# DLRM tower on one core: fifteen tables picked by matmul in place of fourteen, and eight buffers for gathered rows

## The chip, the cores and the metric

One core of one Trainium2 chip. The metric is the device time of one execution in microseconds (us), lower is better. A profiled execution gives a span, from its first to its last recorded instruction, and its own time.

## The reference

For each of 512 samples, 32 rows of 128 numbers are looked up in 32 tables by `ids`. All pairs of these rows are multiplied (a 32 x 32 matrix of dots for a sample, of which the upper triangle is used), 16 context numbers are added, and three layers follow.

```python
e = jnp.stack([tbl_0[ids[:, 0]], ..., tbl_31[ids[:, 31]]], axis=1)   # 512 x 32 x 128
dot = jnp.einsum('bnd,bmd->bnm', e, e)
z = dot[:, iu, ju]                                   # iu, ju = triu_indices(32, k=1)
h = jnp.concatenate([z, dense_ctx], axis=1)          # 512 x 512
h = jnp.maximum(h @ W_top1 + b_top1, 0.0)            # 512 x 512
h = jnp.maximum(h @ W_top2 + b_top2, 0.0)            # 512 x 256
y = h @ W_top3
```

Eleven tables have 1000 rows, twelve have 1250, eight 12500 and one 125000. Everything is float32.

## The kernel before

The embeddings end in `emb`, with the 128 dimensions on the partitions, by one of two ways.

**Picks.** The 14 smallest tables (`PICK`) are read whole, as 8 chunks of 128 rows each (11 tables) or 10 chunks (3 tables), 118 chunks in all. For each chunk there is a mask `onehot`, 128 rows x 512 samples, that is one where a sample's id is that row. TensorE multiplies the chunk by its mask and adds the chunks of a table up in a bank of `two_ps` (L479, L481). A table is split in two parts, `high` and `low`, each multiplied by itself: ScalarE copies `high` (L353), VectorE subtracts `low` = table - high (L275, "the subtraction"). Most masks are made by VectorE (L290, three or four chunks to an instruction), some by ScalarE in two steps, `away` (L373) and `onehot` (L383); the table `BY_ACT` says how many of each table. `onehot` holds 16 chunks, so a mask waits until TensorE has counted up `picked_done` for the chunk that held its place. `pick_out` on ScalarE copies two tables at a time out of `two_ps` when the second is complete. Three tables are held, and SyncE loads the next one (`home<-picked`) when the one three before has been subtracted.

**Gathers.** The other 18 features (`GF`) come as single rows. GpSimd issues an indirect DMA for each tile of 128 rows (L266, 72 of them). The samples are in 4 blocks of 128; a block has 5 banks of tiles, the first of `MORE` = 2 tiles and four of 4 tiles, 20 banks in all (`NB`). TensorE turns a bank by transposes, `turn(k)` (L495), into `turn_ps`, and ScalarE copies it to `emb` (`emb_out(k)`, L353), which counts up `emb_ready`. The tile `rows` holds `ROWS_HELD` = 4 banks: before the gathers of bank k GpSimd waits until `turned` has reached k - 3. In TensorE's order, after the picks of table t comes `turn(t - 1)`, up to bank 12, and behind it bank 13.

**Dots.** For each pair of samples one matmul of 64 columns (L519; the profile has two records for each) gives their 32 x 32 dots. There are 8 groups of 64 samples (64 records each), two to a block, going to `free_ps` and `two_ps` in turn. `dots_out` copies them to `home`, ScalarE the first half of a group and VectorE the second (L179). SyncE stores a block's dots to HBM (`dots_store`, L183) and loads them back as `pairs` (L189), 128 features and context on the partitions.

**Layers.** `layer1(r)` (L528) wants the pairs of block r, and four blocks are put through layer 1, then layers 2 and 3 in three parts. Between them stand the last banks' turns and the dots of groups 6 and 7.

All engines' lists are written by hand, in the order in which the code below stands; they meet by semaphores only.

Of the kernel before, what the change touches and what calls it, by code (L numbers as in the profile page):

```python
# [7 lines left out]
        1250, 12500, 1250, 1250, 1250, 12500, 12500, 1000, 1000, 1000, 1250, 1250, 1000, 1000,  # L8
        1000, 1250, 1250, 1250]

PICK = 14
PICKED = sorted(range(F), key=lambda f: (ROWS[f], f))[:PICK]
GATHERED = [f for f in range(F) if f not in PICKED]
SLOTS = GATHERED + PICKED
# [2 lines left out]
KRMAX = max(KR)  # L17
CHUNK0 = [sum(KR[:t]) for t in range(PICK + 1)]
STEPS = sorted(set(KR))
# [1 line left out]
PIECE = 2  # L21
PIECES0 = KR[0] // PIECE

BY_ACT = [0, 2, 2, 2, 1, 2, 2, 2, 2, 1, 2, 2, 2, 3]

TWOS = -(-PICK // 2)
ACT0 = [sum(BY_ACT[:t]) for t in range(PICK + 1)]

# [8 lines left out]
NB = BLOCKS * BANKS  # L37
TILES = [TB if k % BANKS else MORE for k in range(NB)]
TILE0 = [sum(TILES[:k]) for k in range(NB + 1)]

TURNED = PICK - 1
TABLES_HELD, IDS_HELD, HOT, AWAY, ROWS_HELD = 3, 4, 16, 6, 4

BATCH = 4

# [11 lines left out]
def build(nc, row_ids, pick_ids, tables, picked, context, w1, w2, small, y):  # L57
# [4 lines left out]
    with ctx:  # L62
# [6 lines left out]
        def sem(name):  # L69
            return ctx.enter_context(nc.semaphore(name))  # L70
# [53 lines left out]
        row_ids_in = sem("row_ids_in")  # L124
        pick_ids_in = [sem(f"pick_ids_in{t}") for t in range(PICK)]
        piece_in = [sem(f"piece_in{j}") for j in range(PIECES0)]
# [17 lines left out]
        turned = sem("turned")  # L144
# [31 lines left out]
        def copy_dots(copy, grp, j):  # L176

            at = GRP // 4 * (grp % 2) + GRP // 8 * j
            return copy(dot_sb[:, grp // 2 % 2, :, at:at + GRP // 8],  # L179
                        dot_ps[grp % 2][j][:, :].rearrange("p (g c) -> p c g", c=2 * F))  # L180
# [71 lines left out]
        @block.gpsimd  # L252
        def _(pool):
            for i, k in enumerate(STEPS):
                pool.iota(own_row_i[:, i, 0:k], [[1, k]], base=0, channel_multiplier=k).then_inc(own_rows_made, 1)
            pool.memset(ident[:, :], 0.0).then_inc(ident_ready, 1)
            pool.wait_ge(ident_ready, 1)
            pool.affine_select(out=ident[:, :], in_=ident[:, :], compare_op=ALU.not_equal, fill=1.0,
                               base=0, pattern=[[-1, P]], channel_multiplier=1).then_inc(ident_ready, 1)
            pool.wait_ge(row_no_ready, 1)  # L260
            for k in range(NB):
                if k >= ROWS_HELD:
                    pool.wait_ge(turned, k - ROWS_HELD + 1)
                for i in range(TILES[k]):
                    c = TILE0[k] + i
                    pool.indirect_dma_start(  # L266
                        rows[:, k % ROWS_HELD, i, :], None, tables,
                        bass.IndirectOffsetOnAxis(ap=row_no[:, c:c + 1], axis=0)
                    ).then_inc(rows_in[k % ROWS_HELD], 16)

        @block.vector
        def _(dve):
# [5 lines left out]
            def make_onehots(t, k0, k1):  # L278

                i, k = STEPS.index(KR[t]), k0  # L280
                while k < k1:
                    c = CHUNK0[t] + k
                    n = min(BATCH, k1 - k, HOT - c % HOT)
                    if k1 - k == BATCH + 2:
                        n = min(n, 3)
                    if c + n > HOT:
                        dve.wait_ge(picked_done, c + n - HOT)
                    ids = pick_id[:, t % IDS_HELD, :].unsqueeze(1).broadcast_to([P, n, B])
                    own = own_ps[:, i, k:k + n].unsqueeze(2).broadcast_to([P, n, B])
                    dve.tensor_tensor(onehot[:, c % HOT:c % HOT + n, :], ids, own, ALU.is_equal).then_inc(onehot_dve, n)  # L290
                    k += n
# [19 lines left out]
            for j in range(PIECES0):  # L311
                make_onehots(0, PIECE * j, min(PIECE * (j + 1), KR[0] - BY_ACT[0]))
                dve.wait_ge(high_ready, j + 1)
                split_low(0, PIECE * D * j, PIECE * D * (j + 1))
            for t in range(1, PICK):
# [4 lines left out]
                dve.wait_ge(pick_ids_in[t], 16)  # L320
                make_onehots(t, 0, KR[t] - BY_ACT[t])

# [28 lines left out]
        def _(act):  # L351
# [13 lines left out]
            def make_away(t):  # L365

                i, first = STEPS.index(KR[t]), KR[t] - BY_ACT[t]
                act.wait_ge(pick_ids_in[t], 16)
# [23 lines left out]
            def emb_out(k):  # L392
                act.wait_ge(turned, k + 1)
                r, u = divmod(k, BANKS)
                if u == 0:
                    out = emb[:, BLK * r:BLK * (r + 1), 4 * TB:GF]
                    in_ = turn_ps[k % 2][:, 0:MORE * P].rearrange("p (f b) -> p b f", f=MORE)
                else:
                    b0 = BLK * r + SUB * (u - 1)
                    out = emb[:, b0:b0 + SUB, 0:4 * TB].rearrange("p b (i f) -> p i b f", i=TB)  # L400
                    in_ = turn_ps[k % 2][:, :].rearrange("p (i b f) -> p i b f", i=TB, f=4)
                copy(out, in_).then_inc(emb_ready, 1)

            def dots_out(grp):
                act.wait_ge(dots, 2 * grp + 1)
                if grp >= 4:
                    act.wait_ge(dots_stored[grp // 2 - 2], 64)
                copy_dots(copy, grp, 0).then_inc(dots_act, 1)
# [18 lines left out]
                    make_away(t + 3)  # L427
                    split_high(t + 3)
            emb_out(TURNED)
            dots_out(0)  # L430
            dots_out(1)
            emb_out(TURNED + 1)
            for grp in range(2, 6):
                dots_out(grp)
            for k in range(TURNED + 2, NB - 1):
                emb_out(k)
# [26 lines left out]
        def _(pe):  # L463
            def pick(t):
# [4 lines left out]
                at, out = t % TABLES_HELD, two_ps[t // 2 % 2][:, t % 2, :]  # L469
                own = KR[t] - BY_ACT[t]  # L470
                for k in range(KR[t]):
# [12 lines left out]
            def turn(k):  # L484
                pe.wait_ge(rows_in[k % ROWS_HELD], 16 * sum(TILES[k % ROWS_HELD:k + 1:ROWS_HELD]))
                if k >= 2:
                    pe.wait_ge(emb_ready, k - 1)
                if k == NB - 1:
                    pe.wait_ge(emb_ready, k)
                for i in range(TILES[k]):  # L490
                    bank, at = k % 2, i
                    if k == NB - 1:

                        bank, at = (k + i // 2) % 2, i % 2
                    last = pe.transpose(turn_ps[bank][:, at * P:(at + 1) * P], rows[:, k % ROWS_HELD, i, :], ident[:, :])  # L495
                last.then_inc(turned, 1)
# [25 lines left out]
            def dot_group(grp):  # L522
                dot(grp, 0)
                dot(grp, 1)
# [24 lines left out]
            for t in range(PICK):  # L549
                pick(t)  # L550
                if t:
                    turn(t - 1)
            turn(TURNED)
            pe.wait_ge(pick_emb_ready, TWOS)
            dot_group(0)
            dot_group(1)
            turn(TURNED + 1)
            for grp in range(2, 6):
                dot_group(grp)
            turn(NB - 5)  # L560
            turn(NB - 4)
            pe.wait_ge(weights_in, 64)
            layer1(0)
# [99 lines left out]
```

## Time and profile before

| | |
|---|---|
| Median of 3 runs | 150.77 us (150.52 to 151.89) |
| Profiled execution's own time | 150.31 us |
| Its span | 148.5 us |
| TensorE busy, matmuls (PE) | 119.0 us, 1008 instructions |
| TensorE busy, weight loads (PEld) | 96.8 us |
| VectorE (DVE) busy | 81.2 us |
| ScalarE (ACT) busy | 68.6 us |
| GpSimd (POOL) busy | 76.0 us |
| Mean granted TensorE clock | 0.94 |

Busy times of engines overlap. Matmuls are pipelined and their ends are modelled, so the sum of their durations is more than the time in which they run. "Record" below is one matmul instruction in the trace.

### The profile page before, as it was taken

To read this page: it belongs to the slowest core of one execution; us is meant where nothing else is said; L and a number is where in the kernel's file an instruction comes from. 1 tells how busy PE (TensorE), PEld (TensorE's weight loads), DVE (VectorE), ACT (ScalarE), POOL (GpSimd) and SP (SyncE) were. 2 spreads that over 40 slices of the span, in tenths; PEclk is the share of its full clock that TensorE was granted. 3 is DMA by queue.
4 is the path that set the end of the run, shared out by engine and by line. 5 is a ranking of instruction groups with operands and counts; after the bars stand their busy time and mean duration, and the time that the engine had idled before them with its cause. 6 is when DMAs were issued, how large, how long until landed. Compare 5 with 4: busy or idle time off the path is not lost.

```text
span 148.5 us, 2544 instructions
## 1 busy us (share of the span) xinstructions
PE 119.0 (80%) x1008; PEld 96.8 (65%) x1008; DVE 81.2 (55%) x80; ACT 68.6 (46%) x109; POOL 76.0 (51%) x80
## 2 busy tenths in 40 slices
PE   0195998789999989769599764487499989799993
PEld 0174776476777776545488564276499979699971
DVE  1599997899999999676993000020113041313300
ACT  3359806989998974069961051012024040300032
POOL 3777885747788777848777567506301700000000
PEclk9999999999999999999779969559869999999999
DMA  2797776557647868882212112205425733042000
GB/s 64 187 338 240 283 214 194 124 160 216 206 121 176 272 226 246 233 288 53 53 35 53 53 33 57 53 2 126 114 63 130 188 99 73 4 141 71 4 0 1
DMA packets 10990, 19.29 MB, mean 130 GB/s; under 512 B 2385, under 2 KB 7377, under 8 KB 10978
## 3 DMA queue, kind: packets, MB, share of 16 engines
q1 hardware_dynamic: 8290, 14.01, 32.0%
q0 software_dynamic: 2304, 4.72, 11.6%
q10 hardware_dynamic: 384, 0.39, 0.8%
q8 instruction: 8, 0.13, 0.4%
q14 instruction: 4, 0.03, 0.1%
HBM read 17.02 MB, written 2.13 MB: 129 GB/s over the span
## 4 chain that ended last, share of the span: by engine, by line
PE 65%; issue 14%; DVE 12%; another core or an unknown queue 4%; ACT 2%; DMA 1%; DVEq 0%
PE two_ps L479 16%; PE two_ps L481 13%; DVE onehot L290 9%; PE two_ps L519 8%; PE two_ps L528 8%; PE free_ps L519 7%; PE turn_ps L495 5%; PE free_ps L539 3%; DVE low L275 3%; PE two_ps L539 2%; ACT emb L353 2%; PE two_ps L544 1%; DMA id_sb<-row_ids 1%; PE turn_ps L528 1%
## 5 line engine op out<-in xcount | busy, mean ns | idle before, releaser
L266 POOL DMA_INDIRECT rows<-tables,row_no x72 | 75.1, 1044 | 42.3 <-issue 19.5
L479 PE MATMUL two_ps<-onehot,high 128*128 128x512 f32 x118 | 50.7, 430 | 15.5 <-DVE low L275 6.9
L290 DVE TENSOR_TENSOR onehot<-pick_id,free_ps 128x1536 fp32r<-128x1536 int16 (+2 forms) x30 | 53.1, 1800 | 4.2 <-DMA pick_id<-pick_ids 2.1
L481 PE MATMUL two_ps<-onehot,low 128*128 128x512 f32 x118 | 48.4, 410 | 0.0
L479 PEld LDWEIGHTS two_ps<-onehot,high 128*128 128x128 f32 x118 | 23.5, 199 | 27.0 <-issue 21.1
L481 PEld LDWEIGHTS two_ps<-onehot,low 128*128 128x128 f32 x118 | 23.5, 199 | 4.4
L275 DVE TENSOR_TENSOR low<-home,high 128x1024 fp32r<-128x1024 f32 (+2 forms) x17 | 18.3, 1076 | 3.0 <-ACT high L353 1.6
L519 PE MATMUL two_ps<-emb 128*64 128x64 f32 x240 | 12.8, 263 | 7.8 <-issue 6.8
L353 ACT ACTIVATE high<-home 128x1024 fp32r<-128x1024 f32 (+2 forms) x17 | 15.8, 941 | 4.9 <-DMA home<-picked 4.2
L373 ACT ACTIVATE away<-pick_id,less_row 128x512 f16<-128x512 int16 x25 | 16.7, 715 | 1.4 <-DMA pick_id<-pick_ids 1.4
L179 DVE COPY home<-free_ps 128x512 f32<-128x512 f32 x4 | 2.8, 692 | 26.4 <-remote 24.1
L519 PEld LDWEIGHTS two_ps<-emb 128*64 128x64 f32 x240 | 11.1, 173 | 9.1 <-issue 8.0
L353 ACT ACTIVATE emb<-two_ps 128x1024 f32<-128x1024 f32 x7 | 7.8, 1110 | 18.2 <-remote 12.9
L353 ACT ACTIVATE emb<-turn_ps 128x512 f32<-128x512 f32 (+1 forms) x20 | 10.6, 542 | 11.6 <-PE turn_ps L495 10.9
L519 PE MATMUL free_ps<-emb 128*64 128x64 f32 x272 | 12.1, 249 | 3.6 <-ACT emb L353 2.4
L383 ACT ACTIVATE onehot<-away 128x512 fp32r<-128x512 f16 x25 | 14.3, 622 | 0.0
L519 PEld LDWEIGHTS free_ps<-emb 128*64 128x64 f32 x272 | 11.0, 162 | 4.8 <-ACT emb L353 2.9
L528 PE MATMUL two_ps<-pairs,w_sb 128*128 128x128 f32 x104 | 12.5, 277 | 0.0
L294 DVE TENSOR_SCALAR h<-two_ps,small_sb 128x128 f32<-128x128 f32 x15 | 4.3, 344 | 14.4 <-PE two_ps L528 7.8
L528 PEld LDWEIGHTS two_ps<-pairs,w_sb 128*128 128x128 f32 x104 | 11.9, 192 | 0.1
L495 PE MATMUL turn_ps<-ident,rows 128*128 128x128 f32 x72 | 10.9, 276 | 0.0
L353 ACT ACTIVATE home<-two_ps 128x512 f32<-128x512 f32 x4 | 2.4, 597 | 18.1 <-PE two_ps L519 18.1
(32 smaller groups left out, 46.4 us busy)
## 6 DMA issues: line engine op xcount, KB each, us to landing
home<-picked SPq DMA_DIRECT2D x10, 512.0 KB
home<-picked SPq DMA_DIRECT2D x3, 640.0 KB
pick_id<-pick_ids SPq DMA_DIRECT2D x14, 128.0 KB
dot_out<-home SPq DMA_DIRECT2D x14, 128.0 KB, 2.5
w_sb<-w SPq DMA_DIRECT2D x3, 512.0 KB
rows<-tables,row_no POOLq DMA_INDIRECT x72
pairs<-dot_out SPq DMA_DIRECT2D x14, 64.0 KB, 2.0
home<-picked SPq DMA_DIRECT2D x4, 128.0 KB, 3.9
```

Source lines behind the costliest of these rows:

```text
L266: pool.indirect_dma_start(rows[:, k % ROWS_HELD, i, :], None, tables, bass.IndirectOffsetOnAxis(ap=row_no[:, c:c + 1], axis=0)).then_inc(r ...
L275: dve.tensor_tensor(low[:, at, a:b], table[:, at, a:b], high[:, at, a:b], ALU.subtract).then_inc(low_ready, 1)
L290: dve.tensor_tensor(onehot[:, c % HOT:c % HOT + n, :], ids, own, ALU.is_equal).then_inc(onehot_dve, n)
L353: return act.activation(out, in_, ACT.Copy)
L373: act.activation(away[:, m % AWAY, :], pick_id[:, t % IDS_HELD, :], ACT.Abs, bias=less_row[:, i, k:k + 1]).then_inc(away_ready, 1)
L383: act.activation(onehot[:, c % HOT, :], away[:, m % AWAY, :], ACT.Relu, bias=1.0, scale=-1.0).then_inc(onehot_act, 1)
L479: pe.matmul(out, high[:, at, D * k:D * (k + 1)], onehot[:, c % HOT, :], start=(k == 0), stop=False)
L481: pe.matmul(out, low[:, at, D * k:D * (k + 1)], onehot[:, c % HOT, :], start=False, stop=(k == KR[t] - 1)).then_inc(picked_done, 1)
L495: last = pe.transpose(turn_ps[bank][:, at * P:(at + 1) * P], rows[:, k % ROWS_HELD, i, :], ident[:, :])
L519: last = pe.matmul(out, e, e, start=True, stop=True, tile_position=(0, 64 * h))
L528: last = pe.matmul(h1_ps[r][n], w1_sb[:, c, n * P:(n + 1) * P], pairs[:, r:r + 1, :, c, :], start=(c == 0), stop=(c == PC - 1))
L539: return pe.matmul(h2_ps[part][n], w2_sb[:, c, n * P:(n + 1) * P], h1[:, c, samples(part)], start=(c == 0), stop=(c == N1 - 1))
```

## The change

- The 15 smallest tables are picked: a fourth one of 10 chunks joins, 128 chunks in all. 17 features are gathered, so the first bank of each block has one tile, and there are 68 gathers. `BY_ACT` gets an entry; table 12 gives one more mask to ScalarE, table 13 one fewer. `TWOS` becomes 8, and with it the banks in `two_ps` that dots and layers use swap places.
- `rows` holds 8 banks. GpSimd's gate is four banks behind up to bank 15 (the same as before); banks 16 to 19 wait only until 12 banks are turned.
- Bank 14 is turned behind the picks of the last table with bank 13 ahead of it, and bank 15 follows; then the dots of groups 0 to 5 stand in a row, where before bank 14's turn stood between groups 1 and 2, and bank 15's behind group 5.

```diff
--- before.py
+++ after.py
@@ -8,7 +8,7 @@
         1250, 12500, 1250, 1250, 1250, 12500, 12500, 1000, 1000, 1000, 1250, 1250, 1000, 1000,
         1000, 1250, 1250, 1250]
 
-PICK = 14
+PICK = 15
 PICKED = sorted(range(F), key=lambda f: (ROWS[f], f))[:PICK]
 GATHERED = [f for f in range(F) if f not in PICKED]
 SLOTS = GATHERED + PICKED
@@ -21,7 +21,7 @@
 PIECE = 2
 PIECES0 = KR[0] // PIECE
 
-BY_ACT = [0, 2, 2, 2, 1, 2, 2, 2, 2, 1, 2, 2, 2, 3]
+BY_ACT = [0, 2, 2, 2, 1, 2, 2, 2, 2, 1, 2, 2, 3, 2, 3]
 
 TWOS = -(-PICK // 2)
 ACT0 = [sum(BY_ACT[:t]) for t in range(PICK + 1)]
@@ -39,7 +39,9 @@
 TILE0 = [sum(TILES[:k]) for k in range(NB + 1)]
 
 TURNED = PICK - 1
-TABLES_HELD, IDS_HELD, HOT, AWAY, ROWS_HELD = 3, 4, 16, 6, 4
+TABLES_HELD, IDS_HELD, HOT, AWAY, ROWS_HELD = 3, 4, 16, 6, 8
+
+AHEAD = 4
 
 BATCH = 4
 
@@ -259,8 +261,8 @@
                                base=0, pattern=[[-1, P]], channel_multiplier=1).then_inc(ident_ready, 1)
             pool.wait_ge(row_no_ready, 1)
             for k in range(NB):
-                if k >= ROWS_HELD:
-                    pool.wait_ge(turned, k - ROWS_HELD + 1)
+                if k >= AHEAD:
+                    pool.wait_ge(turned, min(k - AHEAD + 1, max(PICK - 3, k - ROWS_HELD + 1)))
                 for i in range(TILES[k]):
                     c = TILE0[k] + i
                     pool.indirect_dma_start(
@@ -427,10 +429,8 @@
                     make_away(t + 3)
                     split_high(t + 3)
             emb_out(TURNED)
-            dots_out(0)
-            dots_out(1)
             emb_out(TURNED + 1)
-            for grp in range(2, 6):
+            for grp in range(6):
                 dots_out(grp)
             for k in range(TURNED + 2, NB - 1):
                 emb_out(k)
@@ -551,13 +551,10 @@
                 if t:
                     turn(t - 1)
             turn(TURNED)
+            turn(TURNED + 1)
             pe.wait_ge(pick_emb_ready, TWOS)
-            dot_group(0)
-            dot_group(1)
-            turn(TURNED + 1)
-            for grp in range(2, 6):
+            for grp in range(6):
                 dot_group(grp)
-            turn(NB - 5)
             turn(NB - 4)
             pe.wait_ge(weights_in, 64)
             layer1(0)
```

TensorE, behind the last chunk of the last table's picks, before (numbers behind names are buffers; of each turn and each half group of dots the first row stands, not the x3 or x15 that repeat it):

```order
L495 MATMUL turn_ps0<-ident,rows 128x128 [waits emb_ready,rows_in0]
L495 MATMUL turn_ps1<-ident,rows 128x128 [waits emb_ready,rows_in1]
L519 MATMUL free_ps0<-emb 64x64 [waits emb_ready,pick_emb_ready]
L519 MATMUL free_ps1<-emb 64x64 [waits emb_ready]
L519 MATMUL two_ps1<-emb 64x64 [waits emb_ready]
L495 MATMUL turn_ps0<-ident,rows 128x128 [waits emb_ready,rows_in2]
L519 MATMUL free_ps0<-emb 64x64 [waits dots_act,emb_ready]
```

and after:

```order
L495 MATMUL turn_ps1<-ident,rows 128x128 [waits emb_ready,rows_in5]
L495 MATMUL turn_ps0<-ident,rows 128x128 [waits emb_ready,rows_in6]
L495 MATMUL turn_ps1<-ident,rows 128x128 [waits emb_ready,rows_in7]
L519 MATMUL free_ps0<-emb 64x64 [waits emb_ready,pick_emb_ready]
L519 MATMUL free_ps1<-emb 64x64 [waits emb_ready]
L519 MATMUL two_ps0<-emb 64x64 [waits emb_ready]
L519 MATMUL free_ps0<-emb 64x64 [waits dots_act,emb_ready]
```

Three turns (banks 13, 14 and 15) now stand ahead of the first dot where there were two (12 and 13), and none between groups 1 and 2.

VectorE, the last picks, before:

```order
L290 TENSOR_TENSOR onehot<-pick_id,free_ps 128x2048 [waits picked_done]
L275 TENSOR_TENSOR low<-home,high 128x1280 [waits picked_done,high_ready]
L290 TENSOR_TENSOR onehot<-pick_id,free_ps 128x2048 [waits picked_done,pick_ids_in13]
L290 TENSOR_TENSOR onehot<-pick_id,free_ps 128x1536 [waits picked_done]
L179 COPY home<-free_ps 128x64x8 [waits dots]
```

and after:

```order
L277 TENSOR_TENSOR low<-home,high 128x1280 [waits picked_done,high_ready]
L292 TENSOR_TENSOR onehot<-pick_id,free_ps 128x2048 [waits picked_done,pick_ids_in14]
L292 TENSOR_TENSOR onehot<-pick_id,free_ps 128x1536 [waits picked_done]
L181 COPY home<-free_ps 128x64x8 [waits dots]
L181 COPY home<-two_ps 128x64x8 [waits dots]
```

A subtraction and two mask instructions (seven chunks) are added ahead of the first copy of dots.

## Rows read from the trace of the kernel before

**Rows 1.** the page's part 4, the chain by engine.

```profile
PE 65%; issue 14%; DVE 12%; another core or an unknown queue 4%; ACT 2%; DMA 1%; DVEq 0%
```

**Rows 2.** VectorE's timeline: start us, duration us, engine, line, out<-in, [idle before <-releaser].

```profile
61.44 2.29 DVE L290 TENSOR_TENSOR onehot<-pick_id,free_ps 128x2048 fp32r<-128x2048 int16 x1 [1.13 <-PE two_ps L481]
64.30 2.29 DVE L290 TENSOR_TENSOR onehot<-pick_id,free_ps 128x2048 fp32r<-128x2048 int16 x1 [0.57 <-remote]
68.23 1.49 DVE L275 TENSOR_TENSOR low<-home,high 128x1280 fp32r<-128x1280 f32 x1 [1.65 <-ACT high L353]
...
74.04 1.48 DVE L275 TENSOR_TENSOR low<-home,high 128x1280 fp32r<-128x1280 f32 x1
75.44 3.94 DVE L290 TENSOR_TENSOR onehot<-pick_id,free_ps 128x2048 fp32r<-128x2048 int16 x2
97.28 0.69 DVE L179 COPY home<-free_ps 128x512 f32<-128x512 f32 x1 [17.90 <-remote]
```

**Rows 3.** ScalarE's timeline, the same columns.

```profile
64.23 1.14 ACT L353 ACTIVATE emb<-two_ps 128x1024 f32<-128x1024 f32 x1 [6.79 <-remote]
...
78.93 0.60 ACT L353 ACTIVATE emb<-turn_ps 128x512 f32<-128x512 f32 x1 [2.36 <-PE turn_ps L495]
85.62 1.02 ACT L353 ACTIVATE emb<-two_ps 128x1024 f32<-128x1024 f32 x1 [6.10 <-remote]
...
120.20 1.09 ACT L353 ACTIVATE emb<-turn_ps 128x512 f32<-128x512 f32 x2 [5.04 <-PE turn_ps L495]
```

**Rows 4.** TensorE's timeline, around the picks.

```profile
56.66 0.60 PE L495 MATMUL turn_ps<-ident,rows 128*128 128x128 f32 x4
...
83.06 0.39 PE L481 MATMUL two_ps<-onehot,low 128*128 128x512 f32 x1
```

**Rows 5.** windows: stretch, us, then busy us of each engine, granted clock, DMA share, GB/s.

```profile
72.00:76.00 4.00, 3.93 (x11) 3.09 (x12) 4.00 (x3) 4.00 (x8) 3.30 (x3) 0.59 0.19 49
```

**Rows 6.** the chain that ended last, in order of time: start us, us, what.

```profile
86.70 3.54 PE free_ps L519 x63
90.35 1.06 issue
...
97.17 2.63 PE two_ps L519 x44
...
102.51 0.37 issue
...
106.52 3.12 PE two_ps L519 x57
...
113.72 0.81 PE turn_ps L495 x6
...
120.85 1.15 PE free_ps L519 x32
```

**Rows 7.** GpSimd's timeline.

```profile
65.19 0.94 POOL L266 DMA_INDIRECT rows<-tables,row_no  x1 [1.55 <-remote]
...
68.93 1.61 POOL L266 DMA_INDIRECT rows<-tables,row_no  x1 [0.30 <-issue]
...
85.92 0.94 POOL L266 DMA_INDIRECT rows<-tables,row_no  x1 [2.08 <-PE turn_ps L495]
...
94.66 0.94 POOL L266 DMA_INDIRECT rows<-tables,row_no  x1 [0.31 <-issue]
100.79 0.95 POOL L266 DMA_INDIRECT rows<-tables,row_no  x1 [5.19 <-PE turn_ps L495]
...
104.54 0.95 POOL L266 DMA_INDIRECT rows<-tables,row_no  x1 [0.30 <-issue]
...
118.11 0.94 POOL L266 DMA_INDIRECT rows<-tables,row_no  x1 [0.30 <-issue]
```

**Rows 8.** SyncE's queue, its timeline.

```profile
60.00 0.43 SPq L236 DMA_DIRECT2D w_sb<-w  x1
...
114.59 1.74 SPq L189 DMA_DIRECT2D pairs<-dot_out  x4
```

## Prediction, made before the changed kernel was run

> **What bounds the kernel now.** I read the chain of work that ended last by engine first, then the timelines of VectorE, ScalarE, TensorE and GpSimd from 56 to 122 us. The chain is 65% TensorE, but 14% is "issue", time in which an engine waited for nothing that the profile shows, and 4% an unknown releaser [rows 1]. So TensorE's list of work is the path, with holes in it, and the question is what makes the holes. There are three stages.
>
> Up to 83.45 us the picks run at VectorE's pace. A ten-chunk table costs it one subtraction of 1.48 us and seven or eight masks: table 13 runs from 74.04 to 75.44 + 3.94 = 79.38, which is 5.34 us for the subtraction and seven masks [rows 2]. Before that VectorE idled for 1.13, 0.57 and 1.65 us [rows 2]; the last is a wait for ScalarE, which had sat 6.79 us in front of its copy out of `two_ps` [rows 3]. That copy waits only for TensorE's count of table 9, and TensorE had done table 9 before the turn at 56.66 us [rows 4]. The count got out 7 us late.
>
> From 83.45 to 113.72 us stand the dots of three blocks, 384 records. The first 63 take 3.54 us. Then come holes of 1.06 us and the like with at most 5 records between two, until 97.17: 18 records in 6.8 us. A second set begins at 102.51 and ends at 106.52; after it 57 and twice 64 records run without a hole to 113.72, 0.039 us each [rows 6]. GpSimd's rows stand beside this: its gathers run from 85.92 to 95.60 and from 100.79 to 105.49 [rows 7]. The holes end 1.57 and 1.03 us after the last gather of each run. Between 97.17 and 102.51, mostly without gathers, there is no hole. Counts are late in the same places: VectorE's first copy of dots waited 17.90 us and began at 97.28 [rows 2], though the first 63 records were executed by 90.24. I read this as one effect: while gathers follow each other without a pause, what TensorE reports can get out slowly, and after some 64 dense records TensorE itself stands. The cause I can't see; that the two go together I can.
>
> From 113.72 us on comes a tail of 34.8 us, dense on TensorE but for one place: ScalarE's copy of bank 17 began at 120.20 after 5.04 us of waiting [rows 3], and half of the dots of group 6 had to stand behind it until 120.85 [rows 6]. Gathers ran until 119.05 there [rows 7].
>
> **The change, part by part.**
> *One more table.* VectorE gets +5.34 us (the same subtraction and seven masks; tables 12 and 13 swap one mask). Against it: TensorE now ends 4.1 us after VectorE's last mask, since after an idle start it ran partly at the lower clock of 1.2 GHz (granted clock 0.59 between 72 and 76 us, [rows 5]). At 2.4 GHz a chunk takes 0.46 us, its two matmuls of 0.23 (the last of the picks, at 83.06, is released into the turn at 83.29, [rows 4]), and six chunks follow the last mask, 2.8 us, so 1.3 comes back. The idle 3.35 us before table 12 may shrink by nothing or by nearly all of it: with banks 0, 5 and 10 one tile shorter, GpSimd reaches its pauses 1.25 to 4 us earlier, and late counts come out with a pause. Bounds for the end of the picks are thus +0.7 and +4.0; I take +2.5, the end nearer to the pile-up seen, so 86.0.
>
> *Handing over.* Ahead of the first dot TensorE now needs ScalarE's pick copy of one table, its copy of bank 13 and a one-tile turn: about 0.6 (a bank's copy, [rows 3]) + 0.6 + 0.3, against 1.02 for the pair of tables now. With the 2 us by which the count is late (83.45 to 85.62, [rows 3]) I put 3.5 where it was 3.25. The dots start at 89.5, where it was 86.70.
>
> *The gathers.* Each costs 0.94 us and 0.30 before the next, 1.25. Of the 80.6 us between the first, at 3.28, and 83.84 (2.08 before 85.92, [rows 7]), 3.8 are three pauses like the one before 65.19, 70.0 are 56 gathers, and the other 6.8 come from gathers that overlap a subtraction and take 1.6 us or more, as at 68.93. For 68: 3.3 + 85.0 + 6.8 + 0.7 for the new subtraction is 95.8 without a pause. The gates for banks 4, 6 and 12 are the old ones and cost 1.3 us each when they bite; bank 15 needs turn 11. With one to three pauses the gathers end between 97.1 and 99.7; with a late gate at bank 15, later still. I take 99.0. Behind that gate nothing pauses them: banks 16 to 19 have buffers of their own.
>
> A rule on the new subtraction: the gather at 68.93, which meets the subtraction of 68.23 to 69.72, takes 0.67 us more than the others [rows 2, 7]. The Trainium skill ("SBUF — State Buffer", Who interferes with whom) says that a VectorE instruction with two inputs in SBUF and a GpSimd one that reads SBUF shut each other out wholly. By it the price could be up to the whole 1.48 us, and the gathers' end 99.8. The trace, where most of that subtraction is waited out, agrees.
>
> *The dots.* From 89.5 the first 64 records need 3.6 us, to 93.1. Then the slow flow until 99.0 + 1.3 = 100.3: 7.2 us at 18 per 6.8 us, 19 records. Of the other 301 the first 44 go at 0.060 us as they do after the first set of holes (2.63 us for 44, [rows 6]) and 257 at 0.039, together 12.7. The dots end at 113.0, against 113.72 now, with turn 14 among them: **-0.7**. The start hardly matters here. A microsecond later costs 2.6 records, 0.1 us, as long as the dots start before 96. It is the gathers' end plus 14.0 us that sets it.
>
> *The turn before layer 1.* Six transposes in 0.81 us (bank 15's pair and bank 16, [rows 6]) become four: **-0.25**.
>
> *The tail.* No gather runs beside it any more. Bank 17's copy can follow its turn, over at 118.5, at once, as bank 11's did at 78.93 [rows 3, 4]; the second half of the dots of group 6 can begin at 119.6 in place of 120.85: **-1.25**. The rest is TensorE's own work and stays, if the pairs arrive: the load for the second block is issued from 114.59 [rows 8], 7.4 us ahead of its use at 122.0, and shifts with the dots.
>
> Buffers for eight banks cost no time. The new table's 640 KB and mask ids ride on SyncE's queue ahead of the weights, whose last load is issued at 60.00 [rows 8] and is used after 113: 50 us of cover.
>
> **Sum:** -0.7 - 0.25 - 1.25 = -2.2; the pause at bank 6 may fall away with the shorter bank 5, for which I take 0.3 more: -2.5. The span goes from 148.5 to 146.0, the profiled execution's own time from 150.31 to 147.8, and the median, now 0.46 above that, to **148.3 us**.
>
> **The rivals.**
> *Late counts throttle the picks (slower).* Between 63.6 and 83.8 us TensorE idled for some 4 us and ran slowly for 3, so little piled up. The changed kernel has four ten-chunk tables there and no pause. In the slow flow a chunk is reported every 0.7 us (VectorE's releases at 61.44 and 64.30 stand four chunks apart, [rows 2]) where it is executed in 0.46. If that holds, VectorE stalls for free masks, turn 11 comes late, and bank 15's gate opens at 82 where 77 is due. Then 17 gathers of 1.27 end at 103.6 and the dots at 117.6: +3.9 - 1.5, so 153.2 us. It decides from a gate later than 79.6; there the loss has eaten the tail's gain. For it: the 7 us of delay at 57 to 64. Against it: from 65.19 to 79 us gathers ran without a pause and bank 11's copy was still prompt [rows 3].
>
> *The holes belong to the dots, not to the gathers.* Dense, 384 records take 64 x 0.056 + 320 x 0.039 = 16.1 us; the 27.0 us of now hold 0.7 of a turn and 10.2 of loss. If that comes whatever GpSimd does, the dots end at 89.5 + 26.3 = 115.8, the tail's late copy stays, and with -0.25 this is 152.6 us, or 150.8 with the picks at their lower bound. Against it: 185 records without a hole once the gathers were over. The Trainium skill, in the section named above, says that PE never waits on anyone at these ports. By that rule the gathers would have no hold on TensorE; the trace's two sets of holes stand against it.
>
> *No holes at all.* Both sets began 4.4 and 1.7 us after GpSimd had started again behind a wait. If the restart is the trigger, gathers that run on don't hurt. The dots then take 16.1 us from 89.5, to 105.6: -8.1 - 1.5, so 141.2 us. For it: 32 to 53 us, where gathers ran on beside dense picks. Against it: nothing shows that dots go as picks do.
>
> **How the numbers follow.** A measurement of this kernel tells about 1%, 1.5 us, from no change. The forecast has a chance of 0.50 and a range of its own of 146.4 to 150.3 (the gathers' end at 97.1 to 101); 0.38 of it lies under 149.3. Late counts in the picks get 0.20, holes that belong to the dots 0.13, of which nearly half is within 1%, and no holes 0.17, nearly all of it faster. That makes 0.55 faster, 0.20 within 1%, 0.25 slower. The range reaches into the outer cases on both sides: 143.0 to 153.0.
>
> **What the profile of the changed kernel would show.** If I am right: the picks end near 86, the gathers near 99 without a pause from about 77, holes between the dots until a microsecond after the last gather and none after, the dots over at 113, the copy of bank 17 prompt. I am wrong if holes go on after the gathers or are missing beside them, if bank 15's gate opens after 80, or if the pairs of a block arrive later than TensorE asks for them.

## The result, and the profile after

The changed kernel took 155.0 us in the median of 4 runs (154.38 to 156.27), the kernel before 151.33 us beside it: a ratio of 1.0255, 95% interval 1.0162 to 1.0347. It is slower: the whole interval lies above 1, though it reaches below 1.02. Ratios, here and below, compare only runs in the faster of two states that executions of one kernel show, so they can differ a little from the quotient of the medians. The profiled execution took 154.84 us, with a span of 153.0.

From the page of the changed kernel, the granted clock in 40 slices and the chain by engine (the counterparts of [rows 1, 5]):

```profile
PEclk9998699999999999999999965555699999999999
...
PE 48%; DVE 20%; another core or an unknown queue 13%; issue 8%; DMA 4%; ACT 3%; SPq 2%; DVEq 0%
```

The chain has lost TensorE (65% to 48%) and gained an unknown releaser (4% to 13%, 20 us). The clock is at its lower level of 1.2 GHz (0.5) from some 92 to 107 us: TensorE was busy for 1.1 us of the 19 from 85.75 to 104.8.

VectorE's timeline (counterpart of [rows 2]):

```profile
75.39 1.48 DVE L277 TENSOR_TENSOR low<-home,high 128x1280 fp32r<-128x1280 f32 x1
76.79 3.94 DVE L292 TENSOR_TENSOR onehot<-pick_id,free_ps 128x2048 fp32r<-128x2048 int16 x2
108.91 0.69 DVE L181 COPY home<-free_ps 128x512 f32<-128x512 f32 x1 [28.18 <-PE free_ps L519]
```

The masks end at 76.79 + 3.94 = 80.73, 4.0 us sooner than the 79.38 + 5.34 = 84.72 that the added work alone would give: the 3.35 us of idle time that VectorE had before table 12 are gone. Then it stands for 28.18 us until the first dots.

ScalarE's (counterpart of [rows 3]):

```profile
78.07 0.60 ACT L355 ACTIVATE emb<-turn_ps 128x512 f32<-128x512 f32 x1 [3.40 <-remote]
...
88.15 1.02 ACT L355 ACTIVATE emb<-two_ps 128x1024 f32<-128x1024 f32 x1 [6.70 <-remote]
93.09 0.60 ACT L355 ACTIVATE emb<-turn_ps 128x512 f32<-128x512 f32 x1 [3.91 <-remote]
103.21 1.02 ACT L355 ACTIVATE emb<-two_ps 128x512 f32<-128x512 f32 x1 [9.53 <-remote]
104.04 1.64 ACT L355 ACTIVATE emb<-turn_ps 128x512 f32<-128x512 f32 x3
...
124.14 1.08 ACT L355 ACTIVATE emb<-turn_ps 128x512 f32<-128x512 f32 x2 [4.23 <-PE turn_ps L495]
```

These are the rows to look at. 78.07 is the copy of bank 11, 88.15 that of tables 12 and 13, 93.09 that of bank 12, 103.21 that of the last table, 104.04 those of banks 13 to 15, 124.14 those of banks 17 and 18. TensorE's own rows (counterparts of [rows 4, 6]):

```profile
83.64 0.39 PE L481 MATMUL two_ps<-onehot,low 128*128 128x512 f32 x1
...
93.83 1.08 PE L495 MATMUL turn_ps<-ident,rows 128*128 128x128 f32 x4 [8.10 <-issue]
104.81 0.45 PE L495 MATMUL turn_ps<-ident,rows 128*128 128x128 f32 x1 [9.89 <-ACT emb L355]
105.18 3.68 PE L519 MATMUL free_ps<-emb 128*64 128x64 f32 x64
108.65 2.58 PE L519 MATMUL two_ps<-emb 128*64 128x64 f32 x64
111.06 2.03 PE L519 MATMUL free_ps<-emb 128*64 128x64 f32 x64
...
118.62 0.66 PE L495 MATMUL turn_ps<-ident,rows 128*128 128x128 f32 x4
119.86 3.81 PE L528 MATMUL two_ps<-pairs,w_sb 128*128 128x128 f32 x32 [0.58 <-DMA pairs<-dot_out]
...
124.47 2.08 PE L519 MATMUL free_ps<-emb 128*64 128x64 f32 x64
```

The last chunk was executed at 83.64 to 84.03; its count reached ScalarE at 103.2, **19 us later**. Table 13 was done at 78.4, and was seen at 88.1, 9.7 us late; bank 12, turned at 79.0, was seen at 93.1, 14 us late. It began earlier: bank 11 was turned from 72.78 to 73.38, and ScalarE saw that at 78.07, 4.7 us late. TensorE has next to nothing to do meanwhile: bank 14's turn at 93.83 waits for the copy at 93.09, and bank 15's at 104.81 for bank 13's copy, the first of those at 104.04, which stands behind the one of 103.21 in ScalarE's list. GpSimd's timeline (counterpart of [rows 7]):

```profile
54.92 1.18 POOL L268 DMA_INDIRECT rows<-tables,row_no  x1 [1.32 <-remote]
...
78.30 0.94 POOL L268 DMA_INDIRECT rows<-tables,row_no  x1 [0.61 <-remote]
...
98.28 0.94 POOL L268 DMA_INDIRECT rows<-tables,row_no  x1 [0.30 <-issue]
```

From 54.92 on the gathers follow each other 0.30 us apart. The one exception is bank 15's gate: it waits for bank 11's late count too, and opened at 78.30 after 0.61 us. The last gather ended at 99.22, and the last count came out 4 us after that. The dots then ran without one hole, from 105.18 to 118.62. The four parts of the span, before and after:

| us | before | after |
|---|---|---|
| until the end of the picks | 83.45 | 84.03 |
| from there to the first dot | 3.25 | 21.15 |
| dots of three blocks | 27.02 | 13.44 |
| the rest | 34.78 | 34.38 |
| span | 148.5 | 153.0 |

### The profile page after: what moved, and what is told of

Same layout as the page of the kernel before. It is cut to its first block, busy times and chain, and to the rows that moved or that the text cites. A ratio compares the mean times of both kernels' runs of the same rounds, so it can differ in the third digit from the quotient of the medians.

```text
span 153.0 us, 2595 instructions
## 1 busy us (share of the span) xinstructions
PE 117.5 (77%) x1024; PEld 96.8 (63%) x1024; DVE 86.3 (56%) x83; ACT 76.4 (50%) x117; POOL 73.1 (48%) x76
## 4 chain that ended last, share of the span: by engine, by line
PE 48%; DVE 20%; another core or an unknown queue 13%; issue 8%; DMA 4%; ACT 3%; SPq 2%; DVEq 0%
DVE onehot L292 15%; PE two_ps L479 12%; PE two_ps L481 11%; PE two_ps L528 8%; DVE low L277 5%; PE free_ps L519 4%; PE free_ps L539 3%; PE two_ps L519 3%; PE turn_ps L495 2%; ACT emb L355 2%; PE two_ps L539 2%; DMA dot_out<-home 1%; DMA pairs<-dot_out 1%; PE two_ps L544 1%
## 5 line engine op out<-in xcount | busy, mean ns | idle before, releaser
L268 POOL DMA_INDIRECT rows<-tables,row_no x68 | 72.2, 1062 | 25.4 <-issue 18.9
L479 PE MATMUL two_ps<-onehot,high 128*128 128x512 f32 x128 | 54.4, 425 | 12.3 <-DVE low L277 6.1
L292 DVE TENSOR_TENSOR onehot<-pick_id,free_ps 128x1536 fp32r<-128x1536 int16 (+2 forms) x32 | 56.9, 1812 | 1.6 <-DMA pick_id<-pick_ids 1.3
L481 PE MATMUL two_ps<-onehot,low 128*128 128x512 f32 x128 | 52.1, 407 | 0.0
L481 PEld LDWEIGHTS two_ps<-onehot,low 128*128 128x128 f32 x128 | 25.5, 199 | 4.9
L495 PEld LDWEIGHTS turn_ps<-ident,rows 128*128 128x128 f32 x68 | 8.6, 145 | 21.4 <-issue 19.9
L355 ACT ACTIVATE emb<-two_ps 128x1024 f32<-128x1024 f32 (+1 forms) x8 | 11.4, 1425 | 19.1 <-remote 16.2
L355 ACT ACTIVATE emb<-turn_ps 128x512 f32<-128x512 f32 (+2 forms) x20 | 10.8, 553 | 16.9 <-remote 11.6
L385 ACT ACTIVATE onehot<-away 128x512 fp32r<-128x512 f16 x28 | 16.1, 623 | 1.0 <-PE two_ps L481 1.0
L519 PE MATMUL two_ps<-emb 128*64 128x64 f32 x240 | 8.5, 231 | 1.0 <-ACT emb L355 1.0
L519 PEld LDWEIGHTS two_ps<-emb 128*64 128x64 f32 x240 | 8.0, 147 | 1.3 <-ACT emb L355 1.1
```

The lines of the kernel that those rows point to most:

```text
L268: pool.indirect_dma_start(rows[:, k % ROWS_HELD, i, :], None, tables, bass.IndirectOffsetOnAxis(ap=row_no[:, c:c + 1], axis=0)).then_inc(r ...
L355: return act.activation(out, in_, ACT.Copy)
L385: act.activation(onehot[:, c % HOT, :], away[:, m % AWAY, :], ACT.Relu, bias=1.0, scale=-1.0).then_inc(onehot_act, 1)
L479: pe.matmul(out, high[:, at, D * k:D * (k + 1)], onehot[:, c % HOT, :], start=(k == 0), stop=False)
L481: pe.matmul(out, low[:, at, D * k:D * (k + 1)], onehot[:, c % HOT, :], start=False, stop=(k == KR[t] - 1)).then_inc(picked_done, 1)
L519: last = pe.matmul(out, e, e, start=True, stop=True, tile_position=(0, 64 * h))
```

## The experiments

A group is a set of kernels run one after another on one chip with runs of the kernel before. The first comparison, of the section above, is one more such group. The groups fall in two kinds, and no number can be read without this: in four of the seven (the first comparison, 2, 5 and 6) the kernel before takes 151 us, in three (1, 3 and 4) 129 us. Groups 4 and 5 ran on the same chip, so the chip alone does not decide it. I call the first kind *held* and the second *free*, after what their traces show.

| Group | before, us | kernel | us | ratio (95% interval) |
|---|---|---|---|---|
| 1, free | 129.24 | e1: changed, old gate | 133.15 | 1.030 (1.026 to 1.035) |
| | | e2: before, new gate | 128.8 | 0.999 (0.995 to 1.002) |
| | | e3: before, new order | 131.5 | 1.015 (1.008 to 1.023) |
| | | e4: changed, with pauses | 132.93 | one run |
| 2, held | 151.06 | changed kernel | 154.22 | 1.019 (1.011 to 1.026) |
| | | before, for its trace | 150.91 | one run |
| | | e5: fifteenth table alone | 150.66 | 1.001 (0.995 to 1.007) |
| | | e2 again | 156.72 | 1.045 (1.036 to 1.055) |
| 3, free | 129.09 | e1 again | 133.15 | 1.032 (1.022 to 1.042) |
| | | e4 again | 133.1 | 1.029 (1.021 to 1.037) |
| | | e6: plain loads | 133.07 | 1.029 (1.020 to 1.038) |
| | | e7: more counts | 129.13 | 1.003 (0.998 to 1.008) |
| 4, free | 128.85 | changed kernel | 133.61 | 1.034 (1.028 to 1.040) |
| | | e1, third time | 133.33 | 1.037 (1.031 to 1.043) |
| 5, held | 150.85 | e6 again | 134.89 | 0.894 (0.872 to 0.916) |
| | | e1, fourth time | 151.59 | 1.004 (0.999 to 1.010) |
| 6, held | 151.09 | e4, third time | 148.06 | 0.982 (0.978 to 0.985) |
| | | e7 again | 150.96 | 1.004 (0.995 to 1.012) |

**e1: the old gate in the changed kernel.**

```diff
-                    pool.wait_ge(turned, min(k - AHEAD + 1, max(PICK - 3, k - ROWS_HELD + 1)))
+                    pool.wait_ge(turned, k - AHEAD + 1)
```

> The changed kernel with one thing undone: every bank from 4 on waits until the bank four before it is turned, so the gathers of banks 16 to 19 no longer run on unpaused (the eight buffers stay). Theory A (unpaused gathers hold back what TensorE reports, and a pause lets it out): the last pick's count is seen within 3 us of its execution, the dots start at 87 to 89 us instead of 105.2, holes return between the dots, and the time is 149 to 152 us. Rival B (the three turns ahead of the dots, each behind a copy of ScalarE, make the late start): the dots start after 100 us still and the time stays at 154 to 156.

> The changed kernel with the old gate for all banks, for a place where counts come late (before near 151 us): 0.98 to 1.01. Elsewhere 1.03.

Group 1 was a free one, which neither theory had foreseen: 133.15 us, no hole, and no late count. In the held group 5 it was 1.004, as expected. There TensorE's and then GpSimd's timelines read:

```profile
87.06 1.32 PE L519 MATMUL free_ps<-emb 128*64 128x64 f32 x37
89.41 0.34 PE L519 MATMUL free_ps<-emb 128*64 128x64 f32 x3 [1.03 <-issue]
...
100.75 0.38 PE L519 MATMUL free_ps<-emb 128*64 128x64 f32 x2 [1.84 <-issue]
```

```profile
80.89 0.94 POOL L268 DMA_INDIRECT rows<-tables,row_no  x1 [2.07 <-PE turn_ps L495]
...
99.61 0.94 POOL L268 DMA_INDIRECT rows<-tables,row_no  x1 [0.30 <-issue]
```

The gate made pauses (2.07 us before 80.89), the last table's copy began at 85.20, and the dots at 87.06, where the changed kernel began at 105.2. The holes are back: from 89.41 to the row at 102.17 just 19 records pass, and the flow gets free after the gathers' end at 100.55. So with the old gate most of the changed kernel's loss in held groups, 1.9 and 2.6%, is gone. This trace also has a pause of 1.27 us before 67.25, at bank 13's gate, which is the same in both kernels and at which the changed kernel did not stop; the bare pauses of e4 below do not depend on that.

**e2: the new gate in the kernel before.**

```diff
-TABLES_HELD, IDS_HELD, HOT, AWAY, ROWS_HELD = 3, 4, 16, 6, 4
+TABLES_HELD, IDS_HELD, HOT, AWAY, ROWS_HELD = 3, 4, 16, 6, 8
...
-                if k >= ROWS_HELD:
-                    pool.wait_ge(turned, k - ROWS_HELD + 1)
+                if k >= 4:
+                    pool.wait_ge(turned, min(k - 3, max(PICK - 3, k - ROWS_HELD + 1)))
```

> The kernel before with one part of the change alone: eight buffers, and banks 15 to 19 wait only until 11 banks are turned. Picks, tiles and the order of turns and dots are as before. Theory A: counts from TensorE pile up behind the unpaused gathers, the dots start 10 us or more later than at 86.7, close to the end of the gathers, and the time is 153 to 157 us. Rival B (order) and rival C (the fifteenth table does it): no loss, 146 to 151 us.

> The kernel before with eight buffers and the loosened gate alone, again, as a probe for late counts: 128 to 130 us if there are none here; 153 to 157 us and dots that start near the gathers' end if there are.

In group 1 it made no difference (0.999); in group 2 it cost 4.5% (156.72 us, beside 151.06). TensorE's timeline in group 2:

```profile
85.60 1.15 PE L519 MATMUL free_ps<-emb 128*64 128x64 f32 x32 [0.27 <-issue]
...
88.50 0.22 PE L519 MATMUL free_ps<-emb 128*64 128x64 f32 x1 [1.09 <-issue]
...
99.81 0.26 PE L519 MATMUL free_ps<-emb 128*64 128x64 f32 x1 [1.84 <-issue]
...
105.47 0.27 PE L519 MATMUL free_ps<-emb 128*64 128x64 f32 x1 [1.06 <-issue]
106.87 0.27 PE L519 MATMUL free_ps<-emb 128*64 128x64 f32 x1 [1.14 <-issue]
...
108.96 2.97 PE L519 MATMUL two_ps<-emb 128*64 128x64 f32 x63
```

GpSimd's, the last pause and the last gather, and ScalarE's copy of the last two tables:

```profile
71.11 0.94 POOL L266 DMA_INDIRECT rows<-tables,row_no  x1 [1.61 <-PE turn_ps L495]
...
103.41 0.94 POOL L266 DMA_INDIRECT rows<-tables,row_no  x1 [0.30 <-issue]
```

```profile
84.50 1.05 ACT L353 ACTIVATE emb<-two_ps 128x1024 f32<-128x1024 f32 x1 [3.99 <-issue]
```

Here the picks' last count was prompt (the copy at 84.50, the last chunk at 84.07) and the dots started at 85.60, so my expectation was wrong on the place, but they stood just the same: 22 records between 87.09 and 107.6, where I had counted on 2.6 a microsecond. The prompt count matters for the changed kernel: in e2, too, no pause stands behind the last pick, since the gathers run from 71.11 to 104.35. So that missing pause alone does not make the handing over late. What differs is how long the gathers had run by then, 13 us since a pause of 1.61 us here, and 29 us there but for the 0.61 us at 78.30. The flow also gets thinner as the run of gathers grows: near 88 us one or two records come every 0.7 us, near 106 one every 1.4 us. It is free at 108.27, some 4 us after the last gather's end at 104.35.

**e5 and e3: the other parts.** e5 is the changed kernel with four buffers, their gate, and the old order around the dots (bank 15's turn between groups 1 and 2). e3 is the kernel before with bank 14 turned and copied ahead of the dots (TensorE's part of the edit; ScalarE's list is changed to match):

```diff
+            turn(TURNED + 1)
             pe.wait_ge(pick_emb_ready, TWOS)
-            dot_group(0)
-            dot_group(1)
-            turn(TURNED + 1)
-            for grp in range(2, 6):
+            for grp in range(6):
                 dot_group(grp)
```

> The kernel before with the fifteenth table, its masks and the smaller first bank alone: four buffers, gates and the order of dots and turns as before (bank 15 turned between groups 1 and 2). Theory A2 (without late counts the loss is the added table's VectorE work, 5.3 us less what is idle now): 132 to 134 us where before is 129.2. Rival (the order of dots and the pairs' round trip make most of the loss): 130 to 131 us. With late counts present: 149 to 153.

> The kernel before with another part alone: bank 14 is turned ahead of the dots and copied ahead of the copies of dots, so that groups 0 to 5 stand in a row. Gates, buffers and picks as before. Theory A: within 1.5 us of before, 149.5 to 152. Rival B: 2 us or more slower, since TensorE waits for bank 14's gathers and for ScalarE's copy of bank 12 ahead of the first dot.

In the held group 2 the fifteenth table cost nothing (1.001). In its trace the picks end 2.3 us later than before, but the dots start only 0.2 us later, at 86.88: with fifteen tables and the old gate the handing over takes 1.2 us and not 21. At the second call of layer 1 it is 0.6 us behind (122.52, before 121.94). That four gathers fewer pay for the rest is likely, but was not shown.

The order cost 1.5% in the free group 1, 2.3 us, as its rival had it. TensorE's timeline there:

```profile
80.03 1.11 PE L493 MATMUL turn_ps<-ident,rows 128*128 128x128 f32 x4 [2.03 <-DMA rows<-tables,row_no]
```

TensorE waits 2.03 us for bank 14's gathers ahead of the first dot. The order was not run in a held group, and e5 not in a free one.

**The changed kernel in a free group.**

> The changed kernel again, beside new runs of the kernel before. The first four experiments ran where the kernel before takes 129.2 us and shows neither holes between dots nor late counts. If the late counts are what made the change slow, and they are absent here, then what is left is the added table's work: the picks end 4 to 5 us later, and the loss is 2 to 5 us (131 to 134 where before is 129.2). If the late counts are back (before near 151), the changed kernel is at 154 to 156 again and its dots start near the gathers' end.

> The changed kernel a third time, for its time where counts are not late, if this is such a place (before near 129 us). There the gate can't matter, so it should stand where the two kernels with its order and its fifteenth table stood, at a ratio of 1.028 to 1.032, 132 to 134 us. If the loosened gate gains something of its own where counts come at once, it is under 1.02.

The first of the two ran in the held group 2 and took 1.019 times the kernel before. ScalarE's copy of the last table was as late again, and the dots began at 105.09:

```profile
103.12 1.02 ACT L355 ACTIVATE emb<-two_ps 128x512 f32<-128x512 f32 x1 [13.00 <-remote]
```

The second ran in the free group 4. The changed kernel is slower there too, by 3.4%, and as e1 is as slow (1.037 beside it), not by its gate. TensorE's timeline of the changed kernel in group 4:

```profile
82.64 1.03 PE L495 MATMUL turn_ps<-ident,rows 128*128 128x128 f32 x8
84.47 0.30 PE L495 MATMUL turn_ps<-ident,rows 128*128 128x128 f32 x1 [0.79 <-ACT emb L355]
84.70 2.08 PE L519 MATMUL free_ps<-emb 128*64 128x64 f32 x64
...
98.52 3.81 PE L528 MATMUL two_ps<-pairs,w_sb 128*128 128x128 f32 x32 [1.62 <-DMA pairs<-dot_out]
...
103.13 2.09 PE L519 MATMUL free_ps<-emb 128*64 128x64 f32 x64
```

and of the kernel before, for which e7 stands, as fast as it (1.003), in group 3:

```profile
77.15 1.03 PE L496 MATMUL turn_ps<-ident,rows 128*128 128x128 f32 x8
78.45 2.09 PE L520 MATMUL free_ps<-emb 128*64 128x64 f32 x64 [0.27 <-ACT emb L354]
...
92.29 3.81 PE L529 MATMUL two_ps<-pairs,w_sb 128*128 128x128 f32 x32 [0.88 <-DMA pairs<-dot_out]
...
97.85 0.66 PE L496 MATMUL turn_ps<-ident,rows 128*128 128x128 f32 x4 [1.31 <-DMA rows<-tables,row_no]
```

The picks end 5.5 us later (the 8 transposes behind them at 82.64 and 77.15). The dots start 6.25 us later, since TensorE waits 0.79 us for ScalarE's chain ahead of the one-tile turn. Layer 1 starts 6.2 us later, each with some wait for the pairs. Then the kernel before has to wait 1.31 us for gathers (97.85), the changed one no more, and of 6.2 us 4.7 are left: spans of 131.7 and 127.0. Here no late count and no hole hides VectorE, and most of the added 5.3 us comes through. This is read from two timelines; the table alone was not run in a free group. The 2.03 us of e3 are not part of it: the changed kernel has no wait for gathers ahead of its first dot. The second trace of the kernel before, from group 2:

> The kernel before again, for its trace on the same chip. If it takes about 129 us, the picks end near 77.5 us, the dots run at 0.03 us a record without holes although gathers run beside them, and each copy out of a bank starts within 0.3 us of its turn. If it takes about 151 us, holes and late counts are as in the first trace.

It took 150.91 us and had the holes and the late counts again.

**e4: a bare pause.** Ahead of banks 16 to 19, in the changed kernel (the scratch tile `idle` and the semaphore `idled` are new):

```diff
+                if k >= 16:
+                    for j in range(2):
+                        pool.memset(idle[:, :], 0.0).then_inc(idled, 1)
+                        pool.wait_ge(idled, 2 * (k - 16) + j + 1)
```

> The changed kernel, its gates as they are, with some 3 us of other work on GpSimd (two clears of a scratch tile) ahead of the gathers of each of banks 16 to 19. Nothing waits for anything new, there is only a pause. Theory A with the pause as what lets counts out: the last pick's count is seen at the first pause after 84 us, the dots start before 92 us, and the gathers end near 111. If it is the waiting GpSimd and not the pause, or the number of gathers left, counts stay late and the dots start only after 100 us. The time itself may be anything from 150 to 158, since the gathers end later.

> The changed kernel with 3 us of clears on GpSimd ahead of each of banks 16 to 19 and its loosened gate, for a place where counts come late. If a pause in the gathers is what lets counts out, ScalarE's copy of the last table starts before 92 us in place of 103. If only fewer gathers help, it stays behind 100 us. Elsewhere 1.03 as twice before.

In the free groups it took 132.93 us in one run and 133.1 (1.029), like the other kernels with the changed kernel's order and table. In the held group 6 the last table's copy began at 84.72 and not at 103, the dots at 86.58. GpSimd's, ScalarE's and TensorE's timelines there:

```profile
80.45 2.00 POOL L270 MEMSET idle<- 128x1024 f32 x2
82.72 0.95 POOL L274 DMA_INDIRECT rows<-tables,row_no  x1 [0.27 <-POOL idle L270]
```

```profile
84.72 1.06 ACT L361 ACTIVATE emb<-two_ps 128x512 f32<-128x512 f32 x1 [1.80 <-PE two_ps L487]
```

```profile
86.58 1.50 PE L525 MATMUL free_ps<-emb 128*64 128x64 f32 x42
...
95.39 2.23 PE L525 MATMUL free_ps<-emb 128*64 128x64 f32 x50 [1.07 <-issue]
...
111.93 1.12 PE L501 MATMUL turn_ps<-ident,rows 128*128 128x128 f32 x4
```

The two clears took 2.0 us, not 3, and with the idle 0.27 behind them the gathers stand still for 2.3 us. The same gathers, over 9 us later (108.28, not 99.22), and the kernel is **faster** than before by 1.85% (two runs), where the changed kernel was slower by 1.9 and 2.6%. It took 148.06 us, less than the 150 to 158 that I had left open. It is the only kernel with the reference's output that was faster than before in any group. In free groups it is slower than the kernel before. Its gate is still the new one, so it is the pause that lets counts out and not what the gate waits for. (Bank 15's gate, just ahead, cost this kernel 1.16 us and the changed one 0.61.)

It does not keep the holes off. From 86.58 to 111.93 the dots take 25.35 us, where they take 11.35 without holes (e6 below), and holes of 1.0 us and the like return with the gathers. The pauses mended the handing over, not the dots.

**e6: no gathers for banks 16 to 19.** SyncE loads 16 tiles of neighbouring rows of the tables in their place, so the output is not the reference's; GpSimd ends with bank 15, and TensorE's turns of banks 16 to 19 wait for the loads.

```diff
+            sp.wait_ge(turned, PICK - 3)
+            for k in range(16, NB):
+                for i in range(TILES[k]):
+                    sp.dma_start(rows[:, k % ROWS_HELD, i, :], tables[P * (TILE0[k] + i):P * (TILE0[k] + i + 1), :]
+                                 ).then_inc(plain_in[k - 16], 16)
...
-            for k in range(NB):
+            for k in range(16):
```

> The changed kernel with the gathers of banks 16 to 19 (16 tiles) replaced by plain loads of as many rows of the same size from SyncE's hardware queue, behind the same gate; the output is not the reference's, since these rows are the first ones of the tables and not those asked for. GpSimd stops at bank 15. Where counts come late: if GpSimd's gathers hold them up, nothing is late after 80 us, the dots start before 88 us and have no holes, and the time is under 145 us. If any transfer of rows does it, the dots start after 95 us. Where they don't come late: 130 to 133 us.

> Banks 16 to 19 by plain loads from SyncE's queue in place of gathers, again (the same rows of the tables for every sample, so the output is not the reference's), for a place where counts come late. There: if GpSimd's gathers hold the counts, ScalarE's copy of the last table starts by 87 us, no holes between dots, under 145 us. Where before takes 129 us: 1.03 as before.

In the held group 5 this gave 134.89 us, 10.6% under the kernel before, and near its own 133.07 in a free group. GpSimd's last gather, SyncE's queue, ScalarE's copy of the last table, and the dots:

```profile
78.79 0.94 POOL L274 DMA_INDIRECT rows<-tables,row_no  x1 [0.30 <-issue]
```

```profile
77.95 7.47 SPq L243 DMA_DIRECT2D rows<-tables  x16
```

```profile
84.87 1.06 ACT L361 ACTIVATE emb<-two_ps 128x512 f32<-128x512 f32 x1 [0.84 <-PE two_ps L487]
```

```profile
86.73 2.09 PE L528 MATMUL free_ps<-emb 128*64 128x64 f32 x64
...
98.08 0.66 PE L504 MATMUL turn_ps<-ident,rows 128*128 128x128 f32 x4
```

The dots take 11.35 us in place of 27 or 13.4. As many bytes by another queue did not hold the last table's count back, so it is GpSimd's gathers that do. Two limits: the loads read neighbouring rows where gathers read scattered ones, and they were issued from 77.95 to 85.42, beside the last picks. Beside the dots there was next to no load of rows, so for the holes e6 compares gathers with nothing.

**e7: one more count from each of 118 matmuls.**

```diff
                 pe.matmul(out, high[:, at, D * k:D * (k + 1)], onehot[:, c % HOT, :],
-                          start=(k == 0), stop=False)
+                          start=(k == 0), stop=False).then_inc(extra, 1)
```

> The kernel before with 118 more counts from the picks that nobody waits for. Where counts come late (before near 151 us): 154 us or more if the number of counts is what clogs, within 1% of before if not. Elsewhere 1.00 as before.

Nothing in either kind (1.003 and 1.004): the number of TensorE's counts in the picks is not what clogs.

## Why the prediction was wrong

The sign was wrong, and 155.0 lies outside the range of 143.0 to 153.0. By its steps:

- *What bounds the kernel*: right for held groups. Gathers without a pause hold back TensorE's counts (e4, e6) and TensorE itself (e2, e4). In free groups neither is seen, which one trace could not show.
- *One more table*, +2.5 us taken between +0.7 and +4.0: +0.58 measured, a little under the lower bound. VectorE's idle time went whole.
- *The gathers*, end taken at 99.0: 99.22. The gate of bank 15, due at 77, opened at 78.30. The gather at 75.94, beside the last subtraction, took 1.76 us, 0.82 more than the others, where 0.7 was taken.
- ***Handing over*, the step that failed**: 3.5 us taken, 21.15 measured. Of the 3.5, the 1.5 for copies and a turn were near: the free trace of group 4 needs 1.9 (82.80 to 84.70). The other 2, for the late count, were the error; 19 us were measured. I took them over from the kernel before, where the gate of bank 16 made a pause at 83.8, just behind the last pick. In the changed kernel the lateness grows while the gathers run on: 4.7, 9.7, 14 and 19 us for counts executed at 73.4, 78.4, 79.0 and 84.0, and it ends after the last gather. Pauses alone bring the last table's copy from 103.2 to 84.72 (e4), and so does an end of the gathers at 79.73 (84.87, e6). I had written that nothing pauses the gathers behind that gate, and used it for their end only, not for the counts that ScalarE needs in that very stretch. The trouble is older than that gate, though: the gathers had run since 54.92, and e2, paused at 71.11, had its last count at once. How long a run it takes was not settled.
- *"The start hardly matters"*, as long as the dots start before 96: this failed with it, since they start behind the last gather. It also rested on 2.6 records a microsecond in the slow flow; in the long run of e2 it was 1.1, falling to 0.7.
- *The dots*: 13.44 us from 105.18. After a start that late the estimate would be 16.1; it was less since dense records take 0.029 us at 2.4 GHz and 0.054 at 1.2 GHz. The idle wait cost two groups of dots the higher clock (granted 0.50 and 0.75, then 1.00): 3.47 and 2.41 us for 64 records, where the later groups take 1.87, so 2.1 us. The small number is not this step come true: with the start so late the dots had no gathers beside them.
- *The tail*, -1.5 us with the turn taken: -0.4 measured. The copy of bank 17 is prompt now, at 124.14, and that stretch is 0.9 us shorter, where 1.25 was expected. But the dots now follow each other faster than their pairs make the round trip through HBM: TensorE waits 0.58 us at 119.86, which I had named as a sign of being wrong, and the stretch before layer 1 grows by 0.43 where 0.25 was to be saved.
- *The rivals*: late counts were the slower rival's cause, but I placed its price in the picks and at bank 15's gate, with 0.20. The picks ran undisturbed; the price was paid at their end. Its 153.2 us has the right side for a reason that was half right.

In free groups the forecast would have failed in another way: there are no holes to win back, the fifteenth table is paid nearly whole, and a ratio of 1.034 stands.

What stays open: what in a gather holds the counts, and why a chip shows it in one group and not in another. Excluded are the number of TensorE's counts in the picks (e7) and, for the late counts, the bytes as such (e6) and what GpSimd waits for (e4). Whether it matters that the gathered rows are scattered was not tried. Nor was it tried whether it is the making of the gathers' descriptors, their completion, or the records that the profiler takes of both.

## What to carry to other kernels

A run of back-to-back gathers is not only GpSimd's time: look how late other engines see TensorE's counts beside it, and how long the longest run without a pause is. A gate that is loosened "because the buffers are there" can remove the pauses that kept a neighbour alive; 2.3 us without a gather ahead of each of four banks turned a loss of 1.9 to 2.6% into a gain of 1.85% where counts were held, and gave nothing where they were not. Where one trace shows an effect of 20 us that no instruction explains, run the unchanged kernel again in another group of runs before a sum is built on it.

## What the runs showed of the hardware

- The same kernel takes 151 or 129 us, by the group of runs; one chip was seen in both kinds. Late counts and holes beside gathers are seen in the traces of 151 us and not in those of 129.
- In held groups a count of TensorE got out up to 19 us late, and TensorE's 64-column records fell to one in 1.4 us; both ended 1 to 4 us after the last gather. With 2.3 us without gathers, from 80.45 to 82.72, the last table's count was prompt (84.72); the holes came back with the next gathers.
- Sixteen loads of as many bytes by SyncE's queue, from 77.95 to 85.42, held no count back (84.87).
